# A recommendation head on one core: loads, tile 0 and the order of the layers rearranged

## What is computed

```
users, items = interactions[:, 0], interactions[:, 1]         # 2048 pairs
x = concat(users_emb[users], items_emb[items])                # 2048 x 64
h = relu(x @ w1.T + b1)                                       # 2048 x 128
h = relu(h @ w2.T + b2)                                       # 2048 x 128
head_in = concat(one_hot(items, 1250), h)                     # 2048 x 1378
out = sigmoid(head_in @ w_head.T + b_head)                    # 2048 x 1250, float32
```

## Time and profile before

| what | us |
|---|---|
| median of 3 runs | 96.69 |
| lowest and highest | 95.99, 96.86 |
| span of the profiled execution | 65.9 |
| PE busy in the span | 56.0 (85%) |
| DVE, ACT, POOL busy | 43.0, 40.3, 31.2 |
| DMA | 21.85 MB, mean 332 GB/s |
| gathers, item and user rows, median from issue to landing | 5.9 |

### The profile page before, as it was taken

How to read it: one execution, slowest core, us unless ns; L and a number is a source line. 1 busy time by engine, 2 the same in 40 slices (tenths; PEclk the granted TensorE clock), 3 DMA queues, 4 the chain that set the end, 5 groups by cost and what they waited for, 6 DMA issues and landing times.

```text
span 65.9 us, 958 instructions
## 1 busy us (share of the span) xinstructions
PE 56.0 (85%) x284; PEld 44.9 (68%) x284; DVE 43.0 (65%) x111; ACT 40.3 (61%) x91; POOL 31.2 (47%) x38
## 2 busy tenths in 40 slices
PE   1999909799999999999999999999999999993000
PEld 1344207388888888888888888888888878881000
DVE  3811666134558987978879797887978879966000
ACT  0623931424256787777878768787876878978000
POOL 4287688688688678768768868800000000000000
PEclk9999998555599999999999999999999999999955
DMA  0489998998989899999999999999999999999940
GB/s 0 53 321 291 298 350 257 222 343 259 222 283 303 336 382 401 392 406 409 401 410 414 400 426 411 410 413 415 410 402 395 419 404 401 390 346 346 372 145 9
DMA packets 8367, 21.85 MB, mean 332 GB/s; under 512 B 1580, under 2 KB 2476, under 8 KB 8364
## 3 DMA queue, kind: packets, MB, share of 16 engines
q0 software_dynamic: 2816, 10.77, 46.7%
q1 hardware_dynamic: 4972, 10.29, 41.1%
q10 hardware_dynamic: 576, 0.76, 3.8%
HBM read 11.56 MB, written 10.24 MB: 331 GB/s over the span
## 4 chain that ended last, share of the span: by engine, by line
PE 73%; DMA 11%; ACT 2%; DVE 2%; POOL 2%; issue 2%
PE acc L359 47%; DMA rows<-user_rows,idx 8%; PE ps_h L355 6%; PE acc L387 3%; PE acc L390 3%; PE acc L388 3%; PE ps_x L340 3%; PE ps_h L346 3%; DMA idx<-pairs 3%; PE ps_h L345 3%; PE acc L385 2%; POOL rows L181 2%; ACT rows L310 1%; DVE rows L244 1%; PE acc L355 1%
## 5 line engine op out<-in xcount | busy, mean ns | idle before, releaser
L244 DVE TENSOR_TENSOR rows<-acc,rows 128x625 f32<-128x625 f32 (+2 forms) x35 | 25.8, 749 | 5.3 <-PE acc L359 3.2
L310 ACT ACTIVATE rows<-rows 128x625 f32<-128x625 f32 (+2 forms) x35 | 23.3, 678 | 0.9 <-DVE rows L244 0.9
L181 POOL DMA_INDIRECT rows<-item_rows,idx x16 | 15.3, 954 | 6.0 <-issue 4.6
L185 POOL DMA_INDIRECT rows<-user_rows,idx x16 | 15.3, 955 | 4.9 <-issue 4.9
L359 PE MATMUL acc<-bias_parts,bias_sel 128*128 128x512 f32 (+1 forms) x42 | 11.2, 373 | 0.0
L359 PE MATMUL acc<-w_hid_hi,h2T_lo 128*128 128x512 f32 (+1 forms) x39 | 10.5, 376 | 0.0
L296 ACT ACTIVATE h1T<-ps_h,b_sb 128x128 f32<-128x128 f32 x16 | 5.9, 368 | 7.1 <-PE ps_h L346 6.6
L359 PE MATMUL acc<-w_hid_hi,h2T_hi 128*128 128x512 f32 (+1 forms) x39 | 10.0, 365 | 0.0
L300 ACT ACTIVATE h2T_hi<-ps_h,b_sb 128x128 fp32r<-128x128 f32 x15 | 5.5, 369 | 7.1 <-PE ps_h L355 7.1
L359 PE MATMUL acc<-w_hid_lo,h2T_hi 128*128 128x512 f32 (+1 forms) x39 | 9.6, 354 | 0.0
L227 DVE CAST embT<-ps_x 128x128 fp32r<-128x128 f32 x16 | 4.7, 292 | 5.5 <-PE ps_x L340 5.4
(11 more groups left out here) (39 smaller groups left out, 58.1 us busy)
## 6 DMA issues: line engine op xcount, KB each, us to landing
probs<-rows SPq DMA_DIRECT2D x20, 312.5 KB
probs<-rows SPq DMA_DIRECT2D x3, 625.0 KB
probs<-rows SPq DMA_DIRECT2D x6, 256.0 KB
w_hid_f<-w_hiddenT ACTq DMA_DIRECT2D x1, 625.0 KB
rows<-item_rows,idx POOLq DMA_INDIRECT x16, 5.9
rows<-user_rows,idx POOLq DMA_INDIRECT x16, 5.9
probs<-rows SPq DMA_DIRECT2D x2, 113.0 KB
probs<-rows ACTq DMA_DIRECT2D x1, 113.0 KB
```

The lines of the kernel that those rows point to most:

```text
L181: nc.gpsimd.indirect_dma_start(out=rows[:, at + UD:at + ROW], out_offset=None, in_=item_rows, in_offset=bass.IndirectOffsetOnAxis(ap=idx[: ...
L185: nc.gpsimd.indirect_dma_start(out=rows[:, at:at + UD], out_offset=None, in_=user_rows, in_offset=bass.IndirectOffsetOnAxis(ap=idx[:, 2 * ...
L244: nc.vector.tensor_tensor(logits(t, c, n), acc[t % SLOTS][:, c:c + n], logits(t, c, n), ALU.add).then_inc(s_sum, 1)
L310: nc.scalar.activation(logits(t, c, n), logits(t, c, n), ACT.Sigmoid).then_inc(s_prob, 1)
```

## The change

- **Loads.** `w_hid_f` is brought by POOL's queue, ahead of the gathers, where the identity's memset was; DVE does that memset first of all. ACT's queue brings the second half of w1T, b_head, and b1 and b2 as two rows of 128; PE turns these two rows by a transpose into `ps_h`, and DVE copies them to `b12_sb`, behind `bias_lo` and ahead of w1T's split.
- **Warm-up.** 3 calls of 512 columns rather than 6, then calls of 128 columns: 4 once the first bank of `w_hid_hi` is there, 3 once the second is. They write `acc[0]`, not `ps_x`.
- **Tile 0.** PE: transpose, a bias pass over two banks whose sums are written over later, layer 1, bias pass of tile 0, layer 2 (now in `ps_x`), bias pass of tile 1, then the head bank by bank with tile 1's transpose and layers between. DVE and ACT orders follow.
- **Loop.** Transpose and layers are for tile t+1, one ahead, spread between the passes: bias pass, `transpose(t+1)`, hi pass, `layer_1(t+1)`, hi-lo pass, `layer_2(t+1)`, lo pass. DVE: `add_part(t-1,0)`, `split_h2(t)`, `copy_embT(t+1)`, `add_part(t-1,1)`, `split_emb(t+2)`. ACT: `sigmoid(t-1,0)`, `relu_1(t+1)`, `sigmoid(t-1,1)`, `relu_2(t+1)`.
- **End.** The same for tiles 14 and 15: `transpose(LAST)` opens, `next_layer_1(LAST)` follows tile 14's first bank, `layer_2(LAST)` its second.

```diff
-WARM = 6
+WARM = 3
+WARM_SHORT = (4, 3)
...
         def _(pool):
-            nc.gpsimd.memset(ident[:], 0.0).then_inc(s_zero, 1)
+            pool.dma_start(w_hid_f[:], w_hiddenT).then_inc(s_hidden, 16)
             pool.wait_ge(s_zero, 1)
...
         def _(dve):
+            nc.vector.memset(ident[:], 0.0).then_inc(s_zero, 1)
             nc.vector.memset(warm_pe[:], 0.0).then_inc(s_warm_pe, 1)
...
                                     ALU.subtract).then_inc(s_bias_split, 1)
+            dve.wait_ge(s_b12_T, 1)
+            nc.vector.tensor_copy(b12_sb[:], ps_h[:, 0:2]).then_inc(s_b12_sb, 1)
             dve.wait_ge(s_w1, 32)
...
             split_hidden(0)
+            split_emb(0)
+            copy_embT(0)
             split_hidden(1)
-            split_emb(0)
             split_hidden(2)
-            copy_embT(0)
             split_emb(1)
+            split_h2(0)
             copy_embT(1)
-            split_h2(0)
+            add_part(0, 0)
+            add_part(0, 1)
             split_emb(2)
-            add_part(0, 0)
+            split_h2(1)
             copy_embT(2)
-            split_h2(1)
-            add_part(0, 1)
             add_part(0, 2)
             split_emb(3)
-            copy_embT(3)
             for t in range(2, LAST - 1):
-
                 add_part(t - 1, 0)
-                if t + 2 < TILES:
-                    split_emb(t + 2)
                 split_h2(t)
+                copy_embT(t + 1)
                 add_part(t - 1, 1)
-                if t + 2 < TILES:
-                    copy_embT(t + 2)
+                split_emb(t + 2)
             split_h2(LAST - 1)
-            add_rows(LAST - 2)
+            add_part(LAST - 2, 0)
+            copy_embT(LAST)
+            add_part(LAST - 2, 1)
             add_part(LAST - 1, 0)
             split_h2(LAST)
...
-            act.dma_start(b1_sb[:], b1.rearrange("(p a) -> p a", a=1)).then_inc(s_b12, 16)
-            act.dma_start(b2_sb[:], b2.rearrange("(p a) -> p a", a=1)).then_inc(s_b12, 16)
-            act.dma_start(w_hid_f[:], w_hiddenT).then_inc(s_hidden, 16)
+            act.dma_start(w1T_f[K1:2 * K1, :], w1T).then_inc(s_w1, 16)
+            act.dma_start(bias_f[:], bias_v).then_inc(s_bhead, 16)
+            act.dma_start(b12_rows[0:1, :], b1.rearrange("(a p) -> a p", a=1)).then_inc(s_b12, 16)
+            act.dma_start(b12_rows[1:2, :], b2.rearrange("(a p) -> a p", a=1)).then_inc(s_b12, 16)
...
-            for t in range(2, LAST):
-
+            for t in range(2, LAST - 2):
+                sigmoid(t - 1, 0)
                 relu_1(t + 1)
-
+                sigmoid(t - 1, 1)
+                relu_2(t + 1)
+            for t in (LAST - 2, LAST - 1):
                 sigmoid(t - 1, 0)
+                relu_1(t + 1)
                 relu_2(t + 1)
                 sigmoid(t - 1, 1)
...
             pe.wait_ge(s_warm_pe, 1)
-            for _ in range(WARM):
-                nc.tensor.matmul(ps_x[:], warm_pe[:, 0:P], warm_pe[:], start=True, stop=True)
+            warm_up(WARM, BANK)
             pe.wait_ge(s_ident, 1)
+            pe.wait_ge(s_b12, 32)
+            nc.tensor.transpose(ps_h[:, 0:2], b12_rows[:], ident[0:2, 0:2]).then_inc(s_b12_T, 1)
+            for bank, count in enumerate(WARM_SHORT):
+                pe.wait_ge(s_hid_hi, bank + 1)
+                warm_up(count, P)
             transpose(0)
-            pe.wait_ge(s_w1_parts, 2)
-
             pe.wait_ge(s_const, 4)
             pe.wait_ge(s_bias_row, 32)
+            one_pass(0, bias_sel[:], bias_parts, True, True, chunks[:-1])
+            pe.wait_ge(s_w1_parts, 2)
+            layer_1(0)
             bias_pass(0)
-            layer_1(0)
-            bias_pass(1, chunks[:-1])
             pe.wait_ge(s_w2, 16)
             layer_2(0, second_layer(0))
+            bias_pass(1)
+            bank_hi(0, 0)
+
+            pe.wait_ge(s_h2, 1)
             transpose(1)
-
-            pe.wait_ge(s_h1, 1)
+            bank_lo(0, 0)
+            bank_hi(0, 1)
             layer_1(1)
-            bank_head(0, 0)
+            bank_lo(0, 1)
+            bank_hi(0, 2)
+            bank_lo(0, 2)
             layer_2(1)
-            bank_head(0, 1)
-            transpose(2)
-
-            bias_pass(1, chunks[-1:])
-            bank_head(0, 2)
+
             def small_beside_head(t, s):
+                transpose(t + 1)
+                hi_pass(t, s)
                 next_layer_1(t + 1)
-                hi_pass(t, s)
                 hi_lo_pass(s)
-
                 layer_2(t + 1)
-                transpose(t + 2)
                 lo_pass(t, s)
...
+            transpose(LAST)
+            bank_head(LAST - 1, 0)
             next_layer_1(LAST)
-            bank_head(LAST - 1, 0)
+            bank_head(LAST - 1, 1)
             layer_2(LAST)
-            bank_head(LAST - 1, 1)
             bank_head(LAST - 1, 2)
```

More of the change, by code:

```diff
@@ L53, in rec_head_kernel @@
     assert B % P == 0 and H1 == P and H2 == P and 2 * K1 == P and item_rows.shape[1] == ITEM_ROW
-    assert BP * BC == N and TILES > IN_FLIGHT and SPARE >= N and LAST % 2 == 1
+    assert BP * BC == N and TILES > IN_FLIGHT and LAST % 2 == 1
     assert all(parts_until(t) == 2 * t + 3 for t in range(LAST - 1))
@@ L152, in _ @@
             sp.dma_start(idx[:], pairs_v).then_inc(s_idx, 16)
-            sp.dma_start(bias_f[:], bias_v).then_inc(s_bhead, 16)
-            for half in range(2):
-                sp.dma_start(w1T_f[half * K1:(half + 1) * K1, :], w1T).then_inc(s_w1, 16)
+            sp.dma_start(w1T_f[0:K1, :], w1T).then_inc(s_w1, 16)
             sp.dma_start(w2T_sb[:], w2T).then_inc(s_w2, 16)
@@ L295, in relu_1 @@
                 act.wait_ge(s_l1, t + 1)
-                nc.scalar.activation(h1T[:], ps_h[:, 0:P], ACT.Relu, bias=b1_sb[:]).then_inc(s_h1, 1)
+                nc.scalar.activation(h1T[:], ps_h[:, 0:P], ACT.Relu, bias=b12_sb[:, 0:1]).then_inc(s_h1, 1)
             def relu_2(t):
@@ L300, in relu_2 @@
                 nc.scalar.activation(h2T_hi[t % SLOTS][:], second_layer(t), ACT.Relu,
-                                     bias=b2_sb[:]).then_inc(s_h2_hi, 1)
+                                     bias=b12_sb[:, 1:2]).then_inc(s_h2_hi, 1)
                 if t >= 1:
                     act.wait_ge(s_h2_lo, t)
-                nc.scalar.activation(h2T_f[:], second_layer(t), ACT.Relu, bias=b2_sb[:]).then_inc(s_h2, 1)
+                nc.scalar.activation(h2T_f[:], second_layer(t), ACT.Relu, bias=b12_sb[:, 1:2]).then_inc(s_h2, 1)
             def sigmoid(t, i):
@@ L377, in lo_pass, with bank_bias, bank_hi, bank_lo @@
                 one_pass(s, h2T_lo[s][:], w_hid_hi, False, True).then_inc(s_acc, 1)
-            def bank_head(t, i):
+            def bank_bias(t, i):
                 s = t % SLOTS
                 c, n = chunks[i]
-                if t >= SLOTS:
-                    pe.wait_ge(s_sum, parts_until(t - SLOTS))
-                    nc.tensor.matmul(acc[s][:, c:c + n], bias_sel[:], bias_parts[:, c:c + n], start=True, stop=False)
+                pe.wait_ge(s_sum, parts_until(t - SLOTS))
+                nc.tensor.matmul(acc[s][:, c:c + n], bias_sel[:], bias_parts[:, c:c + n], start=True, stop=False)
+            def bank_hi(t, i):
+                s = t % SLOTS
+                c, n = chunks[i]
                 pe.wait_ge(s_h2_hi, t + 1)
                 nc.tensor.matmul(acc[s][:, c:c + n], h2T_hi[s][:], w_hid_hi[:, c:c + n], start=False, stop=False)
+                if t == 0:
+                    pe.wait_ge(s_hid_lo, i + 1)
                 nc.tensor.matmul(acc[s][:, c:c + n], h2T_hi[s][:], w_hid_lo[:, c:c + n], start=False, stop=False)
+            def bank_lo(t, i):
+                s = t % SLOTS
+                c, n = chunks[i]
                 pe.wait_ge(s_h2_lo, t + 1)
@@ L391, in bank_head, with warm_up @@
                                  start=False, stop=True).then_inc(s_bank_acc, 1)
+            def bank_head(t, i):
+                if t >= SLOTS:
+                    bank_bias(t, i)
+                bank_hi(t, i)
+                bank_lo(t, i)
+            def warm_up(count, cols):
+                for _ in range(count):
+                    nc.tensor.matmul(acc[0][:, 0:cols], warm_pe[:, 0:P], warm_pe[:, 0:cols], start=True, stop=True)
             pe.wait_ge(s_warm_pe, 1)
-            for _ in range(WARM):
-                nc.tensor.matmul(ps_x[:], warm_pe[:, 0:P], warm_pe[:], start=True, stop=True)
+            warm_up(WARM, BANK)
             pe.wait_ge(s_ident, 1)
+            pe.wait_ge(s_b12, 32)
[3 more added lines that the diff above has]
+                warm_up(count, P)
             transpose(0)
-            pe.wait_ge(s_w1_parts, 2)
             pe.wait_ge(s_const, 4)
             pe.wait_ge(s_bias_row, 32)
+            one_pass(0, bias_sel[:], bias_parts, True, True, chunks[:-1])
+            pe.wait_ge(s_w1_parts, 2)
+            layer_1(0)
             bias_pass(0)
-            layer_1(0)
-            bias_pass(1, chunks[:-1])
             pe.wait_ge(s_w2, 16)
             layer_2(0, second_layer(0))
```

(18 more changed lines are left out.)

17 lines of the change are left out of this document (9 added, 8 removed).

## The result

The changed kernel takes 105.2 us (104.79 to 105.97, four runs), the kernel before 96.42 in the same measurement (95.99 to 96.86, four runs). The ratio is 1.09, 95% interval 1.0805 to 1.0996: slower by 8.8 us, where 4.4 was forecast, and outside the range of 96.4 to 103.4. Executions of one kernel differ by a per cent or two even on one chip; medians here are of all of them, ratios and their intervals of the faster ones alone.

The account below looks back on a forecast made before the run. Compute and the drain of the stores were taken as nearly level bounds. Loop +5.0, tile 0 -0.6, end +0.6 and stores -0.6 summed to +4.4 on 96.69: 101.1 us, range 96.4 to 103.4.

Parts of the forecast that it names:

- Part 1: Loop: layer 1 waits for copy_embT behind DVE's add and split_h2; 3.26 us a tile for 2.84, +5.0 us.
- Part 2: Loads: gathers keep their start at 2.91, w_hid lands at 5.6, tile 0's rows at 9.1 us.
- Part 3: Tile 0: clock falls but rises earlier; tile 1 ends at 19.7 us, -0.6, bounds -2.6 to +1.65.
- Part 4: End: late layer_1(15) adds +0.6 us, 7.2 from tile 13's lo pass; shorter store tail gives -0.6.
- (a): Rival: no wait arises in the loop, the stores' drain sets the end; 95.8 or 96.7 us, chance 0.18.
- (b): Rival: the loop's wait is there but costs half, 0.21 us a tile; 98.6 us, chance 0.10.
- (c): Rival: POOL's DMA delays gathers up to 1.3 us, clock low through tile 0; 103.4 us, chance 0.06.
- The base: Whole kernel: 30.8 us around the 65.9 us span taken as unchanged, all differences put on the median 96.69.

Follow-up runs that it names:

- e6: Changed kernel with copy_embT ahead of split_h2 but behind the add in DVE's loop: 103.08 us, against 95.77 for the kernel before.
- e13: Changed kernel with transpose(t+1) ahead of the bias pass, copy_embT first on DVE and relu_1 ahead of the sigmoid on ACT: 67.72 us against 66.97 before.
- e4: Changed kernel with copy_embT(t+1) ahead of add_part and split_h2 in DVE's loop: 78.66 us against 66.92 for the kernel before.
- e11: Changed kernel with transpose(t+1) ahead of the bias pass and copy_embT first on DVE: 70.54 us against 67.07 for the kernel before.
- e10: Changed kernel as it is, on a chip where handoffs are on time: 71.3 us against 67.07 for the kernel before, ratio 1.0682.
- e3: Changed kernel with w_hid's DMA back on ACT's queue, behind its four small ones: 70.29 us against 66.92 for the kernel before.
- e15: Changed kernel with b_head's DMA on SP's queue, behind the pairs: 70.21 us against 66.97 for the kernel before.
- e9: Kernel before, unchanged, profiled again: span 65.5 us; the four such runs took 66.72 to 67.20 us.
- e2: Kernel before with only w_hid's DMA moved to POOL, ahead of its memset: 67.03 us against 66.92, ratio 0.999.
- e5: Changed kernel, unchanged, on the chip where the kernel before takes 95.77 us: 104.79 us, ratio 1.0936.
- e8: Kernel of e11 with w_hid's DMA on ACT's queue, where the kernel before takes 95.77 us: 104.02 us, ratio 1.0853.

## Why the prediction was right and where it failed

**Part 1, the loop: right.** Forecast 3.26 us a tile by the closed loop add, split_h2, copy_embT, layer 1; measured 3.31, by these pieces. 12 tiles +5.6 for +5.0, within 3.5 to 6.2. From the lo pass's end (55.59) to layer 1 (56.97) it is 1.38 for the 1.40 worked out; layer 1 that waited takes 0.41 for 0.44. Layer 2 costs 0.33 in this chain against 0.23, where I had added 0.03 for it: that is most of what is missing. e6 shows the cause in part, by one instruction moved (3.11), and e13 by taking it away (2.95). That e4 failed adds a thing that the prediction did not see: ACT's queue closes a second loop of nearly the same length (e11, 3.28), so that opening the first alone does not help.

**Part 2, the loads: right but for one omission.** The first gather was forecast to keep its place at 2.91 and starts at 2.79, w_hid at 5.6 and is there at 5.64. Tile 0's rows: 9.1 forecast (from 8.6), 8.44 in e10, 9.39 in the first profile of the changed kernel. The identity's memset on DVE held up nothing, POOL's issue took 0.71. What was left out is b_head's DMA, moved behind the start of w_hid's transfer: I treated only DVE's wait for b1 and b2. e3 and e15 put it at about 1 us, not clear of noise.

**Part 3, tile 0: the number met by luck, the saving not there.** Tile 1 was to end at 19.7. In e10 its lo pass ends at 19.90, but at 2.4 GHz throughout, after 2.13 us of waiting for the bias rows; the fall of the clock that I expected did not come there. The saving at the higher clock and the omitted wait took each other's place. Other executions with the same start differ: 18.63 in e11 (2.4 GHz, 0.90 of waiting) and 19.96 in e13, where the clock did fall and a bank takes 0.42 and more for 0.23. As a difference the term was wrong: I set it against 20.35 of a profile whose clock had fallen, but in e9 before's tile 1 ends at 18.03, at 2.4 GHz. Even without the wait for the bias rows the changed kernel only comes level (17.69 in e15).

**Part 4, the end: right.** From tile 13's lo pass (in e10 its layer 2 ends at 58.79 + 0.34 = 59.13, and with 0.58 for the lo pass that is 59.7) to 66.93 it is 7.2, as forecast. The tail behind the last sigmoid shrank by 1.5 rather than 0.6: to 3.9, from the 5.4 of e9, or by 1.0 from the 4.9 of the profile before.

All of this gives +4.5 where the sum had +4.4, on the chips where the profile of before was at home. That they are so near is luck in part. Between the two executions e9 and e10 the 5.3 us of span are made of +1.9 in tile 0 (forecast -0.6), +5.6 in the loop (+5.0), +0.6 at the end (+0.6), -1.5 behind the last sigmoid (-0.6), and -1.3 that the sum did not have: in e9 tile 5's gathered rows land only at 23.34, PE runs dry until tile 5's transpose at 23.87, and 12 tiles take 35.4 us, not 34.1. The slower changed kernel has no such wait. In the chain of waits of e9:

```profile
16.93 6.41 DMA rows<-user_rows,idx
...
23.87 0.33 PE ps_x L340
```

Rivals (a) and (b) fall with the pitch of 3.31; (c) falls with e2 and with the gather at 2.79.

**The base: this step failed.** "I take these as unchanged and put every difference on 96.69." The 30.8 us were not around the span: 1.8 or 1.9 lie there in every run. The rest lies inside it, on one chip, where the changed kernel's profile shows late handoffs and before's spans are 93.2 to 94.3. The sum was thus made on a profile that does not belong to the time to be forecast, and what hides what is different there. I can say where most of the further 4.3 us comes from (8.8 less the 4.5 of e10), though it is only argued. With late handoffs the first store is issued only at 43.84, after the last gather, and the DMA line behind it stands mostly at 3 to 6 tenths: no backlog, so nothing gives back what compute loses. From tile 1's hi pass to the last sigmoid's end before took 61.03 - 18.24 = 42.8, e10 66.93 - 17.44 = 49.5. That is 6.7 us of longer compute. Where handoffs are on time, the gathers that before waits for and the drain of the stores hide part of it; without that cover the 6.7 is paid in full. That leaves 2.1 of the 8.8. On the chip with late handoffs the changed kernel needs 99.29 - 48.31 = 51.0 for the same stretch, 1.5 more than in e10, with 1.2 GHz granted in its first 3 us; whether before pays the same there, and where it stands when its handoffs recover, is open without a profile of it. For the argument speaks that e6, measured there, gains most of what its pitch says (1.7 of 2.5). Against it speaks that no run isolates the cover.

## What to carry to other kernels

Before anything is put on a profile, set its span beside its own time: here 1.8 us lie around a span, and 30.8 meant that the profile and the times were of different conditions. When layers are moved one tile ahead, go through each in-order queue for the instruction that now makes an input of the same tile: a copy behind an add that waits for the last pass, or a relu behind a sigmoid, closes a loop, and every such loop has to be opened before the pitch comes down. And a small transfer whose data go through two more steps (split, written back) is worth placing ahead of a big one, not beside it: here that was worth about 1 us.

## What the runs showed of the hardware

In the first measurement and on the chip of e5 to e8, the handoffs from PE to DVE and ACT come late in the first 48 us of the kernel, by 1.9 to 12.3 us in the ones shown above; those to PE arrive within 0.15. The same kernels run 28.7 us longer there (95.77 against 67.07) or 33.5 (104.79 against 71.3). The gathers are issued at the same pace on both kinds of chip (every 1.25 us), so issuing them alone is not the cause, and w_hid's DMA on POOL is not either (e8); the cause is unknown. PE, idle for so long, is granted 1.2 GHz from about 16 us, and 2.4 again from about 51, after it has worked on from 48.

A matmul of layer 1 that had to wait for DVE takes 0.30 in the chain (e10), one that did not 0.07: in e10 its weight load starts only at 24.57, behind the copy, after PEld has idled 0.41 us. In the chains, where handoffs are on time, one from DVE to PE shows as 0.13 or 0.14, from ACT to PE as 0.04, from PE to DVE or ACT as 0.02.
